# Filler matmuls on TensorE in the opening stages, the first square roots on GpSimd, and batch 1's statistics one step later

## The reference

```python
def _gn(v, G=32, eps=1e-05):
    B_, H_, W_, C_ = v.shape
    g = v.reshape(B_, H_, W_, G, C_ // G)
    m = jnp.mean(g, axis=(1, 2, 4), keepdims=True)
    s = jnp.var(g, axis=(1, 2, 4), keepdims=True)
    return ((g - m) / jnp.sqrt(s + eps)).reshape(v.shape)

x = x + _L0_conv_ref(_gn(x), w_in, w_qk, w_out, rel_bias)
x = x + _L1_conv_ref(_gn(x), w_qkv, w_out)
```

## Time and profile before

| what | value |
|---|---|
| median of 3 runs | 162.67 us |
| time of the profiled execution | 163.67 us |
| span of the profiled execution | 161.8 us |
| PE busy | 149.7 us, 93% |
| DVE busy | 110.7 us, 68% |
| ACT busy | 107.7 us, 67% |
| POOL busy | 53.6 us, 33% |

### The profile page before, as it was taken

How to read it: one execution, slowest core, us unless ns; L and a number is a source line. 1 busy time by engine, 2 the same in 40 slices (tenths; PEclk the granted TensorE clock), 3 DMA queues, 4 the chain that set the end, 5 groups by cost and what they waited for, 6 DMA issues and landing times.

```text
span 161.8 us, 4264 instructions
## 1 busy us (share of the span) xinstructions
PE 149.7 (93%) x1578; PEld 129.4 (80%) x1578; DVE 110.7 (68%) x326; ACT 107.7 (67%) x218; POOL 53.6 (33%) x106
## 2 busy tenths in 40 slices
PE   7989798889998999999999899989999998999882
PEld 7469588768698789888899679979999887898751
DVE  1646646985485965487538984998769799699241
ACT  2439215984666698757977789676978788875620
POOL 1202527739952466627684213021300200000000
PEclk9999999999999999999999999999999999999998
DMA  4719800000000000079506850299106970010111
GB/s 130 215 34 320 298 0 6 0 0 0 8 0 0 0 4 2 0 259 219 174 4 257 207 184 4 101 263 265 30 0 259 223 229 10 32 34 2 36 38 65
DMA packets 8244, 15.84 MB, mean 98 GB/s; under 512 B 888, under 2 KB 5368, under 8 KB 7456
## 3 DMA queue, kind: packets, MB, share of 16 engines
q1 hardware_dynamic: 7712, 15.29, 31.4%
q10 hardware_dynamic: 512, 0.28, 0.6%
HBM read 10.31 MB, written 5.26 MB: 96 GB/s over the span
## 4 chain that ended last, share of the span: by engine, by line
PE 72%; DVE 12%; ACT 9%; issue 6%; DVEq 0%
PE bank L584 9%; PE bank L561 7%; PE bank L596 7%; PE bank L615 6%; PE bank L606 6%; PE bank L689 5%; PE bank L679 4%; PE bank L484 3%; PE bank L726 3%; PE bank L573 3%; DVE NM L975 3%; PE bank L751 2%; PE bank L709 2%; ACT QP L1199 2%; PE bank L499 1%
## 5 line engine op out<-in xcount | busy, mean ns | idle before, releaser
L1208 ACT ACTIVATE PT<-bank 128x512 f32<-128x512 f32 x64 | 38.2, 599 | 22.0 <-PE bank L615 12.2
L971 DVE CUSTOM_DVE_ANT_0 SB<-bank,Tk 128x256 f32<-128x256 f32 x64 | 24.5, 421 | 16.7 <-PE bank L584 16.5
L367 POOL TENSOR_SCALAR SB<-SB,NM 128x256 f32<-128x256 f32 x64 | 30.4, 490 | 15.3 <-DVE NM L971 15.0
L975 DVE TENSOR_REDUCE NM<-bank 128x4 f32<-128x512 f32 x32 | 21.9, 683 | 6.2 <-PE bank L596 6.0
L982 DVE TENSOR_TENSOR SB<-bank,NM 128x512 f32<-128x512 f32 x32 | 22.1, 691 | 1.1
L584 PE MATMUL bank<-KH,QM 128*128 128x256 f32 x64 | 21.2, 350 | 1.0 <-ACT QM L1188 1.0
L596 PE MATMUL bank<-K,QP 96*128 96x128 f32 x128 | 21.2, 285 | 1.0 <-ACT QP L1199 0.7
L1199 ACT ACTIVATE QP<-Q,con 96x512 fp32r<-96x512 f32 x32 | 21.3, 716 | 0.0
L615 PE MATMUL bank<-con,SB 128*128 128x128 f32 x128 | 19.9, 278 | 0.0
L596 PEld LDWEIGHTS bank<-K,QP 96*128 96x128 f32 x128 | 17.2, 191 | 3.3 <-issue 1.2
L606 PE MATMUL bank<-con,SB 128*128 128x128 f32 x128 | 19.3, 273 | 0.0
(11 more groups left out here) (142 smaller groups left out, 267.8 us busy)
## 6 DMA issues: line engine op xcount, KB each, us to landing
q_terms<-WQK SPq DMA_DIRECT2D x4, 512.0 KB, 2.8
k_terms<-KHL SPq DMA_DIRECT2D x4, 512.0 KB, 3.8
Q<-q_terms SPq DMA_DIRECT2D x4, 512.0 KB, 5.1
K<-k_terms SPq DMA_DIRECT2D x4, 512.0 KB, 6.5
Tk<-bias_rows SPq DMA_DIRECT2D x4, 384.0 KB, 4.8
X<-x SPq DMA_DIRECT2D x4, 256.0 KB, 3.0
Q<-q_terms SPq DMA_DIRECT2D x4, 256.0 KB, 5.7
K<-k_terms SPq DMA_DIRECT2D x4, 256.0 KB, 7.4
```

Source lines behind the costliest of these rows:

```text
L367: last = nc.gpsimd.tensor_scalar(rows_of, rows_of, -1.0, NM[:, i % 2, 2 * u + nt:2 * u + nt + 1], ALU.mult, ALU.add)
L971: last = V.tensor_tensor_reduce(SB[:, idx % SRING, nt * CH:(nt + 1) * CH], half, Tk[:, u, nt * P:nt * P + CH], 1.0, LOWEST, ALU.add, ALU.m ...
L975: V.tensor_reduce(NM[:, i % 2, 4 * u:4 * u + 4], s[:].rearrange("p (h m) -> p h m", h=4), AX.X, ALU.max).then_inc(max_ready, 1)
L1208: A.activation(PT[:, u, :], bank[Z_BANK + u % 2][:], ACT.Exp, scale=-SCALE if is_a(i) else SCALE).then_inc(p_ready, 1)
```

## The change

Five edits. (1) A function `keep_warm(n)` issues n matmuls of `avg` by `avg` on PE into an unused region: two after `query_key_weights`, two after `bias_rows`, two after a new wait on `xs_ready` ahead of `first_projections`, and three (FILL) in each of steps 0 to 3 after the scores. (2) The roots of batch 0 are made on POOL: DVE adds eps to the variance (128x32, from PSUM), POOL raises all 128x32 elements to -0.5 and signals `rs_ready`; ACT's square root and DVE's reciprocal go. (3) ACT's first small activation is an exponential, and the second is gone, so that ACT loads one table. (4) `small_weights(1)` stands before `first_projections` on PE instead of after them. (5) The part sums of squares of batch 1, its root and its broadcast go back by up to one step on DVE and PE, and with them the projections of batch 1.

```diff
-        TIMES_A = [(range(1, 2), (-6, -4, -5, -5)), (range(2, 3), (-5, -3, -4, -4)), ...
+        TIMES_A = [(range(1, 2), (-5, -3, -4, -4)), (range(2, 3), (-5, -3, -4, -4)), ...
...
+        FILL = 3
...
             def deviation(g):
                 b0, b1 = GROUPS[g]
-                if g == 1:
+                if g == 0:
                     pool.wait_ge(fills, 2)
+                    pool.wait_ge(sd_ready, 1)
+                    nc.gpsimd.tensor_tensor(Rs[:, 0], Sd[:], mhalf[:, 0:1].to_broadcast([P, GRP]), op=ALU.pow).then_inc(rs_ready, 1)
+                    return
...
+            deviation(0)
             pool.wait_ge(xrl_ready, 1)
             center(1)
...
+            def keep_warm(n):
+                for _ in range(n):
+                    nc.tensor.matmul(bank[F_BANK][:, CH:CH + P], avg[:], avg[:], start=True, stop=True)
...
             query_key_weights()
+            keep_warm(2)
             bias_rows()
+            keep_warm(2)
             moments(0, 1, part2_ready, var_done)
             project_a(0, 0)
             moments(1, 0, part_ready, mean_done)
+            small_weights(1)
+            pe.wait_ge(xs_ready, 1)
+            keep_warm(2)
             first_projections(0)
             first_projections(1)
-            small_weights(1)
             for t in range(STEPS):
                 if t < UNITS * BLK:
                     scores(t // BLK, t % BLK)
+                if t < LAG:
+                    keep_warm(FILL)
...
-                if t == 0:
-                    moments(1, 1, part2_ready, var_done)
                 if t == 1:
                     project_a(0, 3)
+                    moments(1, 1, part2_ready, var_done)
+                if t == 2:
                     roots_everywhere(1)
...
                 if step == 3 and g == 0:
-                    dve.wait_ge(sd_ready, 1)
-                    V.reciprocal(Rs[:, 0], Sd[:]).then_inc(rs_ready, 1)
+                    dve.wait_ge(var_done, 1)
+                    V.tensor_scalar(Sd[:], m[:, 256:256 + GRP], EPS, None, ALU.add).then_inc(sd_ready, 1)
...
-            norm_x(1, 2)
             for t in range(STEPS):
...
                 if t == 0:
+                    norm_x(1, 2)
+                if t == 1:
                     norm_x(1, 3)
-                if t == 1:
-                    norm_x(1, 4)
                     value_rows(0)
                 if t == 2:
+                    norm_x(1, 4)
                     small_weights(1)
+                if t == 3:
                     norm_x(1, 5)
-                if t == 3:
                     norm_x(2, 1)
...
-            A.activation(warm[:, 0:1], eps[:], ACT.Sqrt)
+            A.activation(warm[:, 0:1], eps[:], ACT.Exp)
...
-            deviation()
             projected(0, 0)
-            A.activation(warm[:, 1:2], eps[:], ACT.Exp)
             first_high(0)
```

More of the change, by code:

```diff
@@ L108, in build @@
         eps = sb("eps", [P, 1])
-        warm = sb("warm", [P, 2])
+        warm = sb("warm", [P, 1])
         avg = sb("avg", [P, P])
@@ L244, in build @@
         IN_A, IN_B = range(BATCH), range(BATCH, UNITS)
-        TIMES_A = [(range(1, 2), (-6, -4, -5, -5)), (range(2, 3), (-5, -3, -4, -4)), (range(3, BATCH), (-10, -8, -9, -9))]
+        TIMES_A = [(range(1, 2), (-5, -3, -4, -4)), (range(2, 3), (-5, -3, -4, -4)), (range(3, BATCH), (-10, -8, -9, -9))]
         WEIGHTS = (4, 6, 23, 31)
@@ L1092, in squares @@
                 A.activation(Sq[:, b], Xc[:, b], ACT.Square).then_inc(sq_ready, 1)
-            def deviation():
-                act.wait_ge(var_done, 1)
-                A.activation(Sd[:], bank[SUM_BANK[0]][:, 256:256 + GRP], ACT.Sqrt, bias=eps[:]).then_inc(sd_ready, 1)
             def high_weights():
```

## The result

The changed kernel took 168.19 us (median of 4, 166.86 to 168.73) against 163.43 for the kernel before in the same comparison: slower, ratio 1.0367 [1.0237, 1.0496], the brackets being a 95% interval. On another chip it was 167.5 against 163.34, ratio 1.0214 [1.0155, 1.0272]. The ratios here are made from each kernel's undisturbed executions, while the medians hold all of them, so the two can differ. The forecast was 165.8: the direction was right, the size was not, and "within 2%" had been given more chance than slower. The kernel before was itself at 163.43 here and not at the 162.67 on which the forecast stood, so 0.8 of the 2.4 us between forecast and result lie in the base; the change cost 4.8 us by the medians, for a forecast of 3.1.

What follows compares the result with a forecast made beforehand. PE was taken as the bound (busy 149.7 of 161.8 us), so opening delays aren't caught up. Sums of +4.3 (lower clock) and +1.7 (higher) gave a middle of +3.1: median 165.8 us, 8-in-10 range 161.0 to 168.2.

Steps and rivals of the forecast that it cites:

- Part 1: Opening on PE: four fillers ahead of the sums of squares add 1.92 us, about 1.0 at the high clock.
- Part 2: Batch 0's roots on POOL: power of 4.8 us puts XF at 16.0 instead of 10.91, +5.1 us with fillers.
- Part 3: From XF to step 0: table load gone, two fillers added; -0.3 us at the lower clock, -1.3 at the higher.
- Part 4: Steps 0 to 4: twelve fillers, clock rising during step 0; -1.2 us, or -2.3 with the clock high from the start.
- Part 5: Step 8: batch 1's queries completed one step later, masked queries wait for them; +0.7 us, ends 0 and 1.4.
- +4.3 for the lower clock in the opening: Whole kernel: sum of the parts with the lower clock up to step 0, 5.1 - 0.3 - 1.2 + 0.7.
- +1.7 for the higher: Whole kernel: sum with the clock high from about 12 us and kept over PE's wait for XF, 4.6 - 1.3 - 2.3 + 0.7.
- the middle: Whole kernel: +3.1 us, taken between the sums +4.3 and +1.7 because nothing in the trace excluded either.
- the long power's case: POOL's power over 4 us, late code with it or not: 164.2 to 168.2 us, chance 0.60.
- the short power: Rival at batch 0's roots: POOL's power under 1.7 us, hidden under the projection; 160.3 to 163.8 us, chance 0.18.
- Late code on POOL: Rival: POOL's first two-operand instruction can't start before 12.3 us; +1.1 to the sum, 166.9 us; no chance of its own.
- A clock that stays low through all of the steps' fillers: Rival in steps 0 to 4: all twelve fillers cost 0.48 us, sum +9.7, 172.4 us, chance 0.05.

Runs made afterwards that it cites:

- roots_pool: Kernel before with only batch 0's roots as a 128x32 power on POOL and one ACT table load; 166.59 us against 163.55, ratio 1.0213.
- roots_back: Changed kernel with batch 0's root on ACT and reciprocal on DVE again, two table loads; 164.78 us against 163.55 for the kernel before.
- pow8: Changed kernel with POOL's power over 8 of 32 columns and a copy of the other 24; 162.29 us against 163.34 before, ratio 0.9962.
- fill_opening: Kernel before with only the opening's six fillers and small_weights(1) moved; 165.42 us against 163.63, ratio 1.0029.
- no_open: Changed kernel without the opening's six fillers and the wait on xs_ready; 166.16 us against 163.34 for the kernel before, ratio 1.0142.
- after_busy: Changed kernel with seven more PE fillers between small_weights(1) and the wait on xs_ready; 166.19 us against 163.63 before, ratio 1.0209.
- short_after: Changed kernel with batch 0's roots made as for batches 1 to 3 (POOL power over 32x1); 163.88 us against 162.52 before, ratio 0.9897.
- steps_late: Kernel before with batch 1 one step later and three fillers in each of steps 0 to 3; 161.43 us against 163.63, ratio 0.9876.
- after_again: Changed kernel measured once more, unchanged; 167.50 us against 163.34 for the kernel before, ratio 1.0214.
- sweep: Kernel before with eight more POOL instructions at its end, powers of 1 to 32 elements and a subtraction; 162.65 us against 162.52, run once.
- late_only: Kernel before with only batch 1's statistics and projections one step later; 162.48 us against 163.55, ratio 0.9964.
- short_before: Kernel before with batch 0's roots by POOL power over 32x1 and one ACT table load; 164.01 us against 162.52, ratio 1.0118.

## Why the forecast was right in its cause and wrong in its size

**Bound and cause: right.** The power stands alone between the sums and XF, everything behind moves with it, and from step 8 on nothing is caught up: 129.8 us to the end, against 129.2 before. roots_pool (the step alone, +3.0), roots_back (the step undone, 2.9 to 3.5 back) and pow8 (the step shortened, 4.1 to 5.2 back) show it in three ways.

**Part 1, fillers ahead of the sums: right at the lower clock.** +1.92 forecast; fill_opening has XF 1.73 later. With a high opening they cost 0.8 (XF at 14.31, and at 13.49 without them in no_open). Taking them out gave 1.3 us (no_open).

**Part 2, the power: 4.8 us forecast, 5.42 measured.** The slope was read from one element to two, 135 and 148 ns; over longer rows it is 157. Of the two slopes that I had, even the higher gave only 5.14. XF was forecast at 16.0 with the lower clock: after_busy, an execution at that level, has 16.66, the 0.6 us of the power. In the changed kernel's own profile it is 14.31, because there the opening was partly at the higher level. At like clocks XF is 5.75 us later with a low opening (16.66 against 10.91) and 5.3 with a high one (14.31 against 8.99).

**Part 3, XF to step 0: right.** From the timeline of the changed kernel, step 0's first matmul starts at 18.37: 4.06 us behind XF, 4.0 forecast for the lower level. For the higher I had 3.1; pow8, short_after and after_busy, with one table load, take 3.54, and roots_back and steps_late, with two, 3.88. So the load is worth 0.3 on the path, as forecast.

**Part 4, steps 0 to 4: right in size, its cause not shown.** The windows from step 0 to step 6, which hold batch 1's query projection in both kernels (columns as above), in the kernel before:

```profile
15.29:29.17 13.88, 12.25 (x63) 10.41 (x62) 8.22 (x34) 5.12 (x13) 7.18 (x13) 1.00 0.33 112
```

and in the changed kernel:

```profile
18.37:30.91 12.54, 12.05 (x87) 11.44 (x86) 9.23 (x38) 5.85 (x14) 7.43 (x13) 0.89 0.04 11
```

13.88 to 12.54, -1.3 for a forecast of -1.2. The clock rose at about 20.9, in step 1, and at 17.7, ahead of step 0 and of the steps' fillers, in after_again. In before's profile it rose near 24 and in the sweep's near 17, without fillers. That the fillers raise it is therefore not shown, and that the size came out is partly luck.

**Part 5, step 8: right.** 3.39 us from step 6 to step 8 before, 4.27 after: +0.9 for +0.7. PE waits 1.73 us there for the masked queries, and waited 0.74 before:

```profile
33.82 0.68 DVE L910 TENSOR_TENSOR Qst<-bank,QH 128x512 fp32r<-128x512 f32 x1
...
34.53 0.51 ACT L1200 ACTIVATE QM<-Qst,con 128x256 fp32r<-128x256 f32 x1 [0.87 <-DVE Qst L910]
...
35.18 0.35 PE L589 MATMUL bank<-KH,QM 128*128 128x256 f32 x1 [1.73 <-ACT QM L1200]
```

**The step that failed is the last one, from two sums to one number.** I had +4.3 for the lower clock in the opening and +1.7 for the higher, wrote that nothing excluded either, and took the middle. Two things were wrong with the +1.7. It needed the high clock to be kept over PE's wait for XF, and no profile of a kernel with the long power and that wait shows it: the changed kernel's two, no_open's and roots_pool's all have a granted clock of 0.50 from 14.8 to 16 us. And it set a changed kernel at the higher level against a kernel before at the lower one, as if the change made the difference. The kernels late_only and steps_late, with before's opening on PE, have XF at 8.99 and 8.83 when that opening is high. So the high opening comes without the change too; how often each kernel gets it isn't on record. At like clocks XF moves by 5.3 or 5.75 us. The low-clock sum with the measured power (+0.6) and the measured step 8 (+0.2) is 4.3 + 0.8 = 5.1, against medians of +4.8 and +4.2. With the middle, half of the long power's case lay under the 2% line; with that sum, most of it would have lain above, and slower would have been the likeliest class.

The two profiles themselves differ by 3.2 us (165.0 and 161.8: +3.4 at XF, -0.3 to step 0, -1.3 to step 6, +0.9 to step 8, +0.6 behind), which is near the +3.1 of the forecast. That is luck: the 3.4 is a dearer power and an earlier opening, which the change didn't cause. What clock the other three executions (167.78 to 168.73) had in the opening isn't on record.

The rivals: the short power is refuted by its row and by the sweep. The Trainium skill, "GPSIMD Engine Reference", section 3.1, gives about 2.6 cycles of 1.2 GHz an element: the subtraction of 128x512 agrees (2.1 ns an element, 2.5 cycles), the power at 157 ns doesn't, and the measurement decides. Late code on POOL is refuted as well: in the changed kernel the power starts at 8.79, 0.15 us behind DVE's addition, and in short_before at 7.97. Section 2.1 of the same page of the Trainium skill gives about 6 us to a first call after code is loaded; no such gap stood before POOL's first power in these two profiles. A clock that stays low through all of the steps' fillers was not seen: those of steps 1 to 3 took 0.67 us for six instructions in the changed kernel.

**Open.** The single parts add to less than the whole. By the medians it is +3.0 for the roots, +1.8 for the opening's fillers and -2.2 for steps_late, +2.6 together, against +4.2 to +4.8. By the ratios it is 2.1%, 0.3% and -1.2%, 1.2% together, against 2.1% and 3.7% in the two comparisons of the changed kernel. With intervals of 0.6 to 1.3% to either side, the gap to 2.1% is within the noise and that to 3.7% is not. The pause of PE behind step 8 is one candidate for the rest, and it is a rival to part of the loss by the roots too, since roots_pool and the changed kernel both have it in their profiles; no run separates it. A fall of the clock is another, but where it was seen it cost nothing that shows: in no_open's profile, after PE had waited from 31.3 to 33.0 us, 3.8 us ran at about half, and from step 8 (34.41) to the end, less the pause of 2.56, it is 129.1 us, as before (columns as above).

```profile
34.40:38.20 3.80, 3.79 (x29) 2.32 (x29) 2.17 (x9) 1.79 (x4) 1.46 (x3) 0.55 0.00 0
```

## What to carry to other kernels

An operation's price on POOL belongs to the operation and not to the engine: where the trace has it at two sizes, extend that slope, and take the last row's for a floor, because here even that was too low. Work that hides under a matmul today has a limit (1.9 us here), and a move pays off only below it; shrink the tile first (one column of 32 partitions instead of 128x32) and ask then which engine takes it. Here even the short way had XF 0.5 us later than ACT's root. Fillers ahead of a sum that PE is late for cost nearly their full length (1.7 of 1.9 us); where PE waits for another engine anyway they cost little or nothing. And where the clock can differ between two executions of one kernel, price the kernel before and the changed one at the same clock, first the one level and then the other: a sum that gives the changed kernel the higher level and leaves the kernel before at the lower credits the change with luck.

## What the runs showed of the hardware

The power on POOL costs 0.39 us and 157 ns for every element in a partition, from 2 to 32, the same on 32 and on 128 partitions, and the same at its first use.

PE's clock can differ from the opening on between executions in which PE does the same. The medians of the kernel before were 162.5 to 163.6 in the five comparisons, with executions from 161.05 to 165.4 in one of them. The difference shows in the opening: with the same seven fillers, the projection of batch 0 ends at 9.0 in late_only's profile and at 10.88 in that of before. The two levels can be read from durations where the granted clock shows 1.00 from the start: before's profile reads 1.00 throughout its opening, in which the durations are those of the lower level. In the changed kernel's profile it reads 1.00 from 12.0 to 13.5, when PE is idle, and 0.50 from 14.8, when PE starts again; in its second profile (after_again) it reads 0.50 through the same idle stretch.
